# Norms on Pool, silu ahead of side work, high halves deferred and the down projection four pairs behind in a fused attention and mixture-of-experts layer

## What is computed

```python
x = x + attn_a(layernorm(x))      # differential attention, 16 heads, 2 maps each
x = x + ffn(layernorm(x))         # 64 experts, top 8, plus a shared expert
x = x + attn_b(layernorm(x))      # attention between the heads' features, 16 x 16
x = x + ffn(layernorm(x))         # the same feed forward again
# attn_a: o = softmax(q1 k1) v - lam * softmax(q2 k2) v ; o = rms_norm(o, sub_norm_w) * (1 - 0.2) ; o @ w_proj.T + b_proj
# ffn: silu(x @ Ws_up) @ Ws_down + sum_e cw[:, e] * (silu(x @ W_up[e]) @ W_down[e])
# cw: sigmoid(affinity) of the top 8 experts of (affinity + bias), divided by their sum
```

## Time and profile before

| | |
|---|---|
| median of 3 runs | 1163.82 us (1159.25 to 1165.16) |
| profiled execution, its own time | 1170.74 us |
| its span | 1168.9 us |
| busy: PE, DVE, ACT, Pool | 1058.2, 967.8, 910.5, 399.9 us |
| mean granted clock | 0.904 |

### The profile page before, as it was taken

The page is one execution under the profiler, slowest core; times in us unless marked ns, Lnnn a source line. Parts: engine busy times, 40 slices in busy tenths (PEclk is TensorE's granted clock), DMA queues, the critical chain, the costliest instruction groups (busy, mean ns, idle before and its releaser), DMA issues.

```text
span 1168.9 us, 21285 instructions
## 1 busy us (share of the span) xinstructions
PE 1058.2 (91%) x8016; PEld 530.6 (45%) x8016; DVE 967.8 (83%) x1169; ACT 910.5 (78%) x1485; POOL 399.9 (34%) x563
## 2 busy tenths in 40 slices
PE   6379999999999999999998998999889998999998
PEld 3012222222222222222222235767677776777876
DVE  7799999999999999999998724788866987688665
ACT  5169999999999999898998875866756775677665
POOL 3352323223232323232314332364423532352333
PEclk9569999999999999999997867998989898989999
DMA  8901110111011101110010005655557565756773
GB/s 276 290 3 47 48 47 9 41 48 48 12 38 49 47 20 30 49 47 24 27 49 20 3 1 126 171 145 140 135 144 193 132 154 137 190 140 165 187 194 100
DMA packets 80470, 108.89 MB, mean 93 GB/s; under 512 B 23536, under 2 KB 33520, under 8 KB 80368
## 3 DMA queue, kind: packets, MB, share of 16 engines
q1 hardware_dynamic: 70752, 103.07, 33.2%
q10 hardware_dynamic: 9616, 4.46, 1.5%
HBM read 95.57 MB, written 11.93 MB: 92 GB/s over the span
## 4 chain that ended last, share of the span: by engine, by line
PE 41%; DVE 32%; ACT 14%; DMA 5%; issue 4%; POOL 2%; SPq 1%; ACTq 0%; DVEq 0%; POOLq 0%
DVE NEGMAX L1046 22%; PE PS L1300 12%; ACT PR L843 9%; PE PS L1273 6%; PE PS L1403 5%; PE PS L1405 5%; PE PS L1404 5%; DMA GATE<-gate_d 3%; DVE HF L1070 3%; DVE XC L992 2%; PE PS L1246 2%; PE PS L1282 2%; DVE HL L1078 2%; ACT HH L935 1%; ACT PS L942 1%
## 5 line engine op out<-in xcount | busy, mean ns | idle before, releaser
L1046 DVE TENSOR_REDUCE NEGMAX<-PS 128x1 f32<-128x1024 f32 x512 | 586.0, 1216 | 38.3 <-PE PS L1246 37.0
L843 ACT ACTIVATE PR<-PS 128x512 f32<-128x512 f32 x1024 | 544.1, 599 | 73.4 <-PE PS L1273 62.6
L1300 PE MATMUL PS<-PR,VG 128*32 128x256 f32 (+1 forms) x3840 | 337.5, 425 | 9.8 <-ACT PR L843 0.6
L1273 PE MATMUL PS<-QB,KB 32*128 32x512 bf16 x1024 | 286.8, 397 | 2.8 <-ACT PR L843 2.0
L1070 DVE TENSOR_TENSOR HF<-PS,GATE 128x1024 f32<-128x1024 f32 x128 | 156.0, 1222 | 105.0 <-ACT PS L942 72.0
L1246 PE MATMUL PS<-KA,QA 32*128 32x512 bf16 x1024 | 194.7, 401 | 48.6 <-DVE NEGMAX L1046 39.8
L942 ACT ACTIVATE PS<-PS 128x1024 f32<-128x1024 f32 x128 | 129.2, 1010 | 95.4 <-PE PS L1405 94.2
L676 POOL TENSOR_TENSOR ORC<-OSB,MINUS 128x16 f32<-128x16 f32 x32 | 93.7, 2929 | 274.9 <-ACT OSB L863 260.5
L1273 PEld LDWEIGHTS PS<-QB,KB 32*128 32x128 bf16 x1024 | 80.6, 92 | 227.0 <-ACT PR L843 155.7
L753 POOL TENSOR_TENSOR HL<-HF,HH 128x1024 fp32r<-128x1024 f32 (+1 forms) x46 | 104.8, 2280 | 178.5 <-ACT HH L935 178.2
L935 ACT ACTIVATE HH<-HF 128x1024 fp32r<-128x1024 f32 (+1 forms) x136 | 139.7, 1028 | 25.8 <-DVE HF L1070 24.8
(11 more groups left out here) (178 smaller groups left out, 855.9 us busy)
## 6 DMA issues: line engine op xcount, KB each, us to landing
GATE<-gate_d SPq DMA_DIRECT2D x256, 256.0 KB, 4.1
QA<-q_stack SPq DMA_DIRECT2D x64, 128.0 KB, 2.6
QB<-q_stack SPq DMA_DIRECT2D x16, 256.0 KB, 2.9
KB<-k_stack SPq DMA_DIRECT2D x16, 256.0 KB, 2.9
KA<-k_stack SPq DMA_DIRECT2D x60, 64.0 KB, 2.4
q_stack<-PARTS SPq DMA_DIRECT2D x12, 256.0 KB, 4.5
k_stack<-PARTS SPq DMA_DIRECT2D x12, 256.0 KB, 4.4
RAWU<-in_L_ffn_W_up_dram ACTq DMA_DIRECT2D x4, 512.0 KB, 11.1
```

Source lines behind the costliest of these rows:

```text
L843: nc.scalar.activation(PR[:, s % PRING, r, :], PS[:, SCORE_BANK[n], :], ACT.Exp, scale=SCALE_A).then_inc(p_ready, 1)
L1046: nc.vector.tensor_reduce(NEGMAX[:, hs % 2, col:col + 1], PS[:, e:e + 2, :].rearrange("p b n -> p (b n)"), axis=AX_X, op=ALU.max, negate=T ...
L1273: mm(PS[:, SCORE_BANK[n], :], KB[strip, u, mt * P:(mt + 1) * P], QB[strip, u, half * BANK:(half + 1) * BANK], start=True, stop=True).then_ ...
L1300: last = mm(PS[STRIP * r:STRIP * (r + 1), 7, cols], VG[:, u, mt, r // 2, :], PR[:, s % PRING, r, cols], start=mt == 0, stop=mt == TB - 1 a ...
```

## The change

- `LAG` is 4, so HH and HL have five places; HF keeps four (`FPLACES`).
- `norm` after attention is done by Pool, right behind the root in `stats`, as two tensor_tensors of 128x512 with broadcast operands; the one norm inside attention stays on DVE. DVE waits before it reuses the statistics' two slots.
- Head norms are done by Pool for each half group (`heads_norm`, eleven instructions); the final product with `sub_norm_w` is `heads(b)`. The stages `rms_*` go. In Pool's loop `shift_parts` stands ahead of `output`, and the loop runs to the last half.
- `neg_lam` is computed by Pool behind the low halves of the weights.
- The affinity inside attention uses exp(-a) on ACT and 1 / (1 + e) on DVE instead of sigmoid.
- ACT does `silu(g)` ahead of `side`, and the high halves by a list: none in a step with an affinity, one in each of the two next steps, then two until it has caught up. DVE and Pool follow the same list with the low halves; Pool takes none of the first six and none at or right after `stats`.
- `up(0)` stands ahead of the last weighted values and `up(1)` ahead of the last output tile, `silu(0)` and `silu(1)` likewise on ACT. DVE's wait for all outputs goes; the other buffers are laid out behind the whole attention area.
- `mix_out` and `mix_back` move from SP to ACT; CWT, GRAM, GK and VMIX have one slot. Stages shift by a step or two in SIDE.

```diff
-LAG = 3
+LAG = 4
 HPLACES = LAG + 1
+FPLACES = 4
...
-    NQ - 28: [("rms_squares", 0), ("rms_sums", 0)], NQ - 26: [("rms_root", 0)], NQ - 25: [("rms_scale", 0)],
-    NQ - 11: [("heads_T", 0)], NQ - 10: [("proj", 0), ("stats", ("f", 0))], NQ - 9: [("norm", ("f", 0))],
-    NQ - 8: [("x_T", ("f", 0))], NQ - 7: [("affinity", 0)], NQ - 6: [("top", 0)], NQ - 5: [("sum", 0)], NQ - 3: [("gate_T", 0)],
+    NQ - 12: [("heads_T", 0)], NQ - 11: [("proj", 0), ("stats", ("f", 0))], NQ - 10: [("norm", ("f", 0))],
+    NQ - 8: [("x_T", ("f", 0))], NQ - 7: [("affinity", 0)], NQ - 6: [("top", 0)], NQ - 5: [("sum", 0)], NQ - 4: [("gate_T", 0)],
...
-    also((n + 1, 9), ("x_T", ("f", f)))
+    also((n + 1, 10), ("x_T", ("f", f)))
...
-    also((n + 1, 10), ("affinity", f))
-    also((n + 1, 11), ("x_T", ("f", f + 1)))
+    also((n + 1, 11), ("affinity", f))
+    also((n + 1, 12), ("x_T", ("f", f + 1)))
...
-    also((n + 1, 12), ("top", f))
+    also((n + 1, 13), ("top", f))
...
-    also((n + 1, 13), ("sum", f))
+    also((n + 1, 14), ("sum", f))
     also((n + 1, 15), ("gate_T", f))
...
+def splits():
+
+    order, late, since = [], 0, 0
+    for g in range(2 * NCH * WIDES):
+        now = []
+        if works(divmod(g, WIDES), ("affinity",)):
+            since = 0
+        elif g:
+            since += 1
+            now = list(range(late, min(late + (1 if late == g - 1 or since < 3 else 2), g)))
+            late += len(now)
+        order.append(now)
+    return order + [list(range(late, 2 * NCH * WIDES))]
...
+def low_on_pool(k):
+
+    g = SPLIT_AT[k]
+    here = divmod(g, WIDES)
+    busy = works(here, POOL_SIDE) or works(divmod(g - 1, WIDES), ("stats",))
+    return k >= POOL_BUSY and not busy and (works(here, DVE_SIDE) or g % 3 == 0)
...
+            def norm(key):
+
+                n, c = LN[key], chunk_of(key)
+                rows, whole = slice(4 * c, 4 * c + 4), [P, 4, DIM]
+                pool.wait_ge(ln_r_ok, n + 1)
+                link(nc.gpsimd.tensor_tensor(XC[:, rows, :], X[:, rows, :],
+                                             ln_mv[:, n % 2, :, 0].unsqueeze(2).to_broadcast(whole), op=ALU.subtract))
+                nc.gpsimd.tensor_tensor(XC[:, rows, :], XC[:, rows, :],
+                                        ln_inv[:, n % 2, :].unsqueeze(2).to_broadcast(whole), op=ALU.mult).then_inc(ln_xn, 1)
...
+            pool.wait_ge(lam_exp, 1)
+            link(nc.gpsimd.tensor_tensor(neg_lam[:], lam_e[:, 1:2], lam_e[:, 0:1], op=ALU.subtract))
+            link(nc.gpsimd.tensor_scalar(neg_lam[:], neg_lam[:], -LAMBDA_INIT, None, ALU.add))
...
+            def heads_norm(k):
+
+                o = O[:, k // 2, 4 * (k % 2):4 * (k % 2) + 4, :].rearrange("p t (h v) -> p (t h) v", v=VD)
+                pool.wait_ge(o_done, k + 1)
+                link(nc.gpsimd.tensor_tensor(rms_q[:], o, o, op=ALU.mult))
+                link(nc.gpsimd.tensor_tensor(rms_q[:, :, 0:4], rms_q[:, :, 0:4], rms_q[:, :, 4:8], op=ALU.add))
+                link(nc.gpsimd.tensor_tensor(rms_q[:, :, 0:2], rms_q[:, :, 0:2], rms_q[:, :, 2:4], op=ALU.add))
+                link(nc.gpsimd.tensor_tensor(rms_v[:], rms_q[:, :, 0], rms_q[:, :, 1], op=ALU.add))
+                link(nc.gpsimd.tensor_scalar(rms_v[:], rms_v[:], 1.0 / VD, EPS_A, ALU.mult, ALU.add))
+                link(nc.gpsimd.tensor_tensor(rms_r[:], rms_v[:], POWER[:].to_broadcast([P, 8]), op=ALU.pow))
...
+                link(nc.gpsimd.tensor_tensor(o, o, rms_r[:].unsqueeze(2).to_broadcast([P, 8, VD]), op=ALU.mult))
...
-            for hs in range(1, 2 * NG - 2):
+            for hs in range(1, 2 * NG):
+                shift_parts(hs)
                 if hs >= 2:
                     output(hs - 2)
-                shift_parts(hs)
...
+                if 2 <= hs < 2 * NG - 1:
+                    heads_norm(hs - 2)
+                if hs == 2 * NG - 3:
+                    heads(0)
...
+                        if isinstance(where, int):
+                            nc.scalar.activation(EX, AFF, ACT.Exp, scale=-1.0).then_inc(ex_ok, 1)
+                        else:
+                            nc.scalar.activation(EX, AFF, ACT.Sigmoid).then_inc(ex_ok, 1)
...
+            silu(0)
+            evac_out(NQ + 1)
+            silu(1)
+            copy_out(2 * NG - 1)
             for g in range(2 * NCH * WIDES):
                 n, w = divmod(g, WIDES)
                 if n and w == LAG:
                     chunk_sum(n - 1)
+                if g > 1:
+                    silu(g)
                 side((n, w))
-                silu(g)
-                if g:
-                    high(g - 1)
-            high(2 * NCH * WIDES - 1)
+                for k in SPLITS[g]:
+                    high(k)
...
-            dve.wait_ge(o_done, 2 * NG)
...
             pe.wait_ge(w_lo, 4)
             pe.wait_ge(xl_ok, 1)
-            pe.wait_ge(m_free, len(ITEM))
+            pe.wait_ge(*evacuated(("gate_T", 0)))
             up(0)
+            for h in range(2):
+                weighted_values(NQ - 1, h)
+            up(1)
             out_tile(2 * NG - 1)
-            pe.wait_ge(p_ready, len(TILE))
             for g in range(2 * NCH * WIDES):
                 n, w = divmod(g, WIDES)
+                if g == 1:
+                    pe.wait_ge(p_ready, len(TILE))
```

More of the change, by code:

```diff
@@ L212, in is_full @@
     return g % WIDES < FULL
-DVE_SIDE = ("proj", "stats", "norm", "y_T", "out_b", "top", "sum", "rms_sums")
-POOL_SIDE = ("stats", "x_T", "affinity", "top", "sum", "rms_scale")
+DVE_SIDE = ("proj", "stats", "y_T", "out_b", "top", "sum")
+POOL_SIDE = ("stats", "x_T", "affinity", "top", "sum", "heads")
+POOL_BUSY = 6
 def works(where, stages):
     return any(st[0] in stages for st in SIDE.get(where, ()))
-def low_on_pool(g):
-    n, w = divmod(g + 1, WIDES)
-    return works((n, w), DVE_SIDE) and not works((n, w), POOL_SIDE) or not works((n, w), POOL_SIDE) and w % 3 == 0
+def splits():
[10 more added lines that the diff above has]
+    return order + [list(range(late, 2 * NCH * WIDES))]
+SPLITS = splits()
+SPLIT_AT = {k: g for g, now in enumerate(SPLITS) for k in now}
+def low_on_pool(k):
[3 more added lines that the diff above has]
+    return k >= POOL_BUSY and not busy and (works(here, DVE_SIDE) or g % 3 == 0)
 def lows_before(g, pool):
@@ L719, in side @@
+                    if stage == "heads":
+                        heads(arg)
                     elif stage == "x_T" and arg[0] == "f":
@@ L725, in side @@
                         root_of(arg)
+                        if not isinstance(where, int):
+                            norm(arg)
                     elif stage == "affinity":
@@ L767, in _ @@
                 side((n, w))
-                if g and low_on_pool(g - 1):
-                    low(g - 1)
-            if low_on_pool(2 * NCH * WIDES - 1):
-                low(2 * NCH * WIDES - 1)
+                for k in SPLITS[g]:
+                    if low_on_pool(k):
+                        low(k)
+            for k in SPLITS[-1]:
+                if low_on_pool(k):
+                    low(k)
         @block.scalar
@@ L917, in side @@
                                   PS[:, bank, :].rearrange("p (j i) -> p i j", i=S0))
-            for s in range(NQ):
-                exp_quad(s)
-                side(s)
-            evac_out(NQ + 1)
-            copy_out(2 * NG - 1)
+                    elif stage == "mix_out":
+                        act.wait_ge(*evacuated(("v_all", 2 * arg + 1)))
+                        act.dma_start(mixed_d[arg].rearrange("i d a j -> (d a) i j"), VP[:]).then_inc(mix_w[arg], 16)
+                    elif stage == "mix_back":
+                        act.wait_ge(mix_w[arg], 16)
+                        if arg:
+                            act.wait_ge(*evacuated(("out_b", 1)))
+                        act.dma_start(RT[:], mixed_d[arg].rearrange("i d a j -> (i d) (a j)")).then_inc(mix_r[arg], 16)
             def high(g):
@@ L952, in chunk_sum @@
                 nc.scalar.activation(YS[:], PS[:, DOWN_BANK, :], ACT.Copy).then_inc(y_evac, 1)
+            for s in range(NQ):
+                exp_quad(s)
+                side(s)
+            silu(0)
+            evac_out(NQ + 1)
+            silu(1)
+            copy_out(2 * NG - 1)
             for g in range(2 * NCH * WIDES):
@@ L1166, in _ @@
                     gated(g)
-                if g and not low_on_pool(g - 1):
-                    low(g - 1)
-            if not low_on_pool(2 * NCH * WIDES - 1):
-                low(2 * NCH * WIDES - 1)
+                for k in SPLITS[g]:
+                    if not low_on_pool(k):
+                        low(k)
+            for k in SPLITS[-1]:
+                if not low_on_pool(k):
+                    low(k)
             side((2 * NCH, 0))
@@ L1388, in side @@
                         pe.wait_ge(*evacuated(("x_T", ("b", arg))))
-                        last = chunk(VMIX[:, arg // 2, :], arg)(bank)
+                        last = chunk(VMIX[:], arg)(bank)
```

(4 more changed lines are left out.)

215 lines of the change are left out of this document (88 added, 127 removed).

## The result

The changed kernel takes 1145.94 us (median of 4 runs, 1143.42 to 1149.39) against 1164.49 us; the ratio is 0.9847, 95% interval 0.9812 to 0.9883. Forecast were 1117.7 us and a range of 1099 to 1140. The direction was right. 18.6 us were gained where 46.1 were forecast, and the result lies above the range. The profiled execution has a span of 1144.3 us, against 1168.9 before. The profiled execution of before was 6.2 us slower than the median of its runs, that of after 0.4 us.

What follows compares the result with a forecast made beforehand. DVE's row maxima were taken to bound attention, PE the feed forward. Terms 5.4 + 6.4 + 4 + 5.4 + 24 + 0.9 = 46.1 us off the 1163.8 us median gave 1117.7; range 1099 to 1140.

Steps and rivals of the forecast that it cites:

- Head norms on Pool, -6.4: Attention, stretch of 622 us: 11 of 33 lost exponentials regained, 6.4 us; Pool's added 5.0 us hidden behind the maxima.
- Rival (3): Slower: Pool becomes the bound of attention through its chain of split, output and head norms; 1211 us at 16 us; chance 0.03.
- Tail, -4: End of attention: split ahead of last outputs, two table loads saved, x_T later; most low clock stays; -4 us (0 to -10).
- rival (1): PE keeps its high level in the tail (-10) and the body is almost clean (-32): 1102 us; chance 0.15.
- Start, -5.4: Start of feed forward: DVE no longer waits for Pool's output; third silu 8.7 us after last exponential instead of 14.1; -5.4 us.
- Body, -24: Feed forward body: 40 us of stalls, most at norms on DVE, less 16.4 us of new delays; -24 us (-12 to -32).
- (a): Feed forward delay: affinity one step behind x_T, whose evacuation now follows silu; 3.0 us in all.
- (c): Feed forward delay at the softmax: its exponential follows silu and DVE waits in line; 1.2 us.
- (e): Feed forward delay: gates of a new chunk, the copy of the routing weights one us later; 0.5 us thrice.
- (b): Feed forward delay: gate_T(4) and (6) now one step behind their sum; 0.85 us each, 1.7 in all.
- (f): Feed forward delay: Pool takes no low half at steps with statistics, so DVE has backlogs at seven places; 7 us.
- rival (2): Body gives only -10: contention moves to Pool's norms and low halves, PE waits for evacuations behind silu; 1132 to 1141; chance 0.25.

Runs made afterwards that it cites:

- norm_dve: The changed kernel with the feed forward's norms back on DVE, two steps behind their statistics: 1149.56 us, ratio 0.9893.
- silu_last: The changed kernel with silu(g) behind the side work of its step on ACT, as before: 1128.60 us, ratio 0.9700.
- first_soft: respace_last with silu ahead of the side work at the two softmax steps alone: 1119.93 us, ratio 0.9642.
- rl_bias_late: respace_last with Pool's addition of the bias for chunk 2 and its transposes two steps later: 1112.76 us, ratio 0.9584.
- neglam_pool: The kernel before with one edit, neg_lam computed on Pool behind the differences of the weights: 1161.22 us, ratio 0.9968.
- att_only: The change's attention side (neg_lam, head norms, tail, start) with the feed forward of the kernel before: 1139.57 us, ratio 0.9795.
- respace_last: The changed kernel with silu behind the side work and the routing chain spread, each sum two steps or more ahead of its gate_T: 1118.10 us, ratio 0.9598.
- att_pool: att_only with the norms of the feed forward on Pool, at the step of their statistics: 1134.32 us, ratio 0.9747.

## Why the prediction was wrong

- **neg_lam, -5.4:** 3.3 us measured by itself, interval 1.9 to 5.7. Mechanism right, the forecast near the upper end of the interval.
- **Head norms on Pool, -6.4:** mechanism right, the size not measured by itself. The stretch has its 33 exponentials. Instructions of Pool in order of time, first, power and last of the eleven:

```profile
694.48 0.29 POOL L706 TENSOR_TENSOR rms_q<-XT 128x64 f32<-128x64 f32 x1
...
696.05 1.66 POOL L711 TENSOR_TENSOR rms_r<-rms_v,POWER 128x8 f32<-128x8 f32 x1
...
699.11 0.30 POOL L716 TENSOR_TENSOR XT<-XT,rms_r 128x64 f32<-128x64 f32 x1
```

  4.9 us for all, 1.66 for the power; estimated were 5.0 and 1.7. Rival (3), Pool as the bound, is out: 50% busy.
- **Tail, -4:** too small, with a reason that holds in part. I held that narrow products mean the low level. In after the clock was 0.91 and 1.00 (windows above); in norm_dve, silu_last, first_soft and rl_bias_late too it was at 1.00 from 679 us on. In the ten other profiles with this attention code the low level did come, for 10 to 14 us, until the first wide products of the feed forward, and the last exponential ended only a little later (683.0 to 684.4 us instead of 680.1 to 683.0). From neglam_pool's last exponential (698.2) to that of after (683.0) are 15.2 us for head norms and tail, where 10.4 were forecast, and some 14 in the ten. So a piece of rival (1) came true, but not reliably. Which edit made the tail shorter wasn't tried alone; in neglam_pool, with the tail of before, 680 to 700 us still show 0.50.
- **Start, -5.4:** right. The third silu comes 7.1 us after the last exponential in after and in the four like it, 8.1 to 9.3 us in the ten others (forecast 8.7, before 14.1). The four terms of attention and start together were 21.2; att_only, which has these and no other part of the change, gives 24.4, of which 3.6 lie in the body.
- **Body, -24: the step that failed.** It came out at +6. The mis-sized term is what the change delays. Against 40 us of relief I set 16.4 us of delays (the 0.2 us for mix_back are not in that sum), and 5.9 of these were for later evacuations and closer places. (a) "affinity stands one step behind x_T", 3.0, and (c) softmax, 1.2: silu first costs 17 us, some 10 of them at affinity steps. I counted silu first as a gain for gating and its cost as the lateness of one evacuation; in fact the order makes ACT idle until up is done, ahead of work that was ready, and moves both table loads in between two silus. It also makes the gates of a new chunk late, (e), 1.5 in the sum: 8.3 us of DVE's time in after, inside the same 17. (b) "gate_T(4) and (6) now one step behind their sum", 0.85 each: these two measured 4.81 and 3.95 us, a third at chunk 2 that I had not seen 3.73, and the clock fell to 0.66 behind the longest; spacing gives 10.5 back. I priced the sum itself, not the queue in front of it on DVE, and for chunk 2 on Pool. After to respace_last are 27.8 us, where 5.9 stood for these terms.
- **The relief** in the body was smaller than 40 as well, by less. Respace_last has no silu first and no sum one step ahead of its gate_T, so by my terms its body would be 40 - 10.5 = 29.5 us shorter than before; it is 24.6 shorter (412.2 against 436.8). Nor did it come from where I looked: the norms on DVE, which I priced at some 31 us, give 5.3 when moved alone (att_pool) and 12.6 in respace_last.
- **(f), low halves beside Pool's norms:** DVE got less relief than I thought, mostly by the rule for the low halves. Groups of DVE over the body, kernel before:

```profile
L1078 DVE TENSOR_TENSOR HL<-HF,HH 128x1024 fp32r<-128x1024 f32 x87 | 112.1, 1290 | 18.7 <-ACT HH L935 18.3
L992 DVE TENSOR_SCALAR XC<-X,ln_mv,ln_inv 128x128 f32<-128x128 f32 x44 | 31.4, 776 | 0.0
```

  and after, where the second is gone:

```profile
L1106 DVE TENSOR_TENSOR HL<-HF,HH 128x1024 fp32r<-128x1024 f32 x97 | 127.9, 1324 | 15.4 <-ACT HH L956 15.4
```

  Ten more low halves fall to DVE by the new rule, so that of 31.4 us only 15.6 are relieved. On average a low half takes only 0.03 us more, but the average hides that the contention was handed over. Instructions of Pool and DVE at one norm in after:

```profile
896.80 1.04 POOL L628 TENSOR_TENSOR XC<-X,ln_mv 128x512 f32<-128x512 f32 x1
...
896.87 2.05 DVE L1106 TENSOR_TENSOR HL<-HF,HH 128x1024 fp32r<-128x1024 f32 x1
...
897.92 1.90 POOL L630 TENSOR_TENSOR XC<-XC,ln_inv 128x512 f32<-128x512 f32 x1
```

  The low half takes 2.05 us instead of 1.22, and Pool's second instruction 1.90 instead of 1.04. A low half is held up like this at eight of the eleven norms, which costs DVE 6.3 us in all. The sign "low halves on DVE take over 2 us beside Pool's norms" so came true at seven of them, and the first part of rival (2) with it. The Trainium skill (SBUF — State Buffer, Who interferes with whom) says that the second to start blocks; the trace agrees, here and at 909.34, where a low half starts beside Pool's addition and takes 2.07 us. But only one low half meets each norm, so the 18 us that I worked out from the rule as an upper bound, 11 more than in the sum, were not reached.
- **End, -0.9:** nothing. 11.1 us from the last silu to the end before, 11.3 after.
- **The rivals.** What happened is rival (2), "PE waits for evacuations behind silu", but at +6 us in the body where I gave it -10, and with a gain in attention that I had in rival (1). Its chance was 0.25 and its bound, 1141, was drawn by the bounds of the single terms; none of them held a wait for a whole queue. Of the other signs, Pool over 90% busy and a wait of PE for XT or RT over 1 us did not come (0.8 us for XT at most). With silu behind the side work and the routing chain spread the changed kernel takes 1118.1 us. That this equals the forecast is partly chance: the forecast had 5.9 us of delays in it that this kernel does not have, and the relief was smaller by nearly as much.

## What to carry to other kernels

On an engine with one queue, don't put an instruction that waits for a product not yet finished ahead of work whose product is ready; above all not where table loads follow. Price a step that is moved next to its consumer by all that stands in front of it in its queue, on every engine that it passes, and add something for the clock that falls behind the wait (about 1 us on 4.8 here). Edits that add slack (another buffer, a deferred half, another engine) can each measure as 0 to 5 us when added to the first version and as 12 to 15 us when taken out of the best, so do both.

## Unexpected of the hardware

PE's clock did not always stay low with narrow products. Windows of after, around the wait of gate_T for Pool:

```profile
672.00:675.00 3.00, 1.28 (x10) 0.62 (x12) 0.77 (x3) 1.45 (x4) 2.05 (x3) 0.84 0.00 0
675.00:678.00 3.00, 3.00 (x28) 0.57 (x20) 0.00 (x0) 1.67 (x4) 2.56 (x6) 0.59 0.19 44
678.00:681.00 3.00, 2.44 (x31) 0.64 (x29) 0.00 (x0) 2.93 (x7) 2.44 (x8) 1.00 0.68 159
```

The gap is like that of the earlier trace rows (1.54 busy of 3.00 us) and the fall behind it too, but 3 us later the clock is at 1.00 again, with the same products running, where before it stayed at 0.50 for 27 us. In respace_last, whose attention code is the same as that of after and whose gap is too (1.28 busy from 670 to 673), it stays at 0.50 from 673 to 685 us. att_only, a window from its profile:

```profile
680.00:690.00 10.00, 9.85 (x60) 4.44 (x52) 1.23 (x1) 6.48 (x10) 2.23 (x6) 0.65 0.53 110
```

So the level behind a gap is not given by the gap or by the kind of product alone: the same code shows both, five profiles of 15 the short fall and ten the long one. The third silu starts at 687.1 to 690.1 us in the five and at 691.1 to 693.4 in the ten, so the fastest kernels here should not be told apart by a few microseconds. What ends the low level was not settled.
